# Moving the first addition of each tile's squares from GpSimd to VectorE, in a Mamba-2 block with routed experts

## What is computed

```
xn = layernorm(x)
z, xBC, dt = split(xn @ in_proj_w.T)             # 1024, 1280, 16 columns
xBC = silu(conv_b + 4-tap causal convolution of xBC)
x_, B, C = split(xBC);  dt = softplus(dt + dt_bias)
y = scan over chunks (decays from dt and A_log)  + x_ * D_skip
y = y * silu(z)
y = y * rsqrt(mean(y*y over its 1024 columns) + 1e-5) * norm_w
out = x + y @ out_proj_w.T + top-2-of-8 experts of xn
```

## Time and profile before

| | |
|---|---|
| median of three runs | 690.48 us |
| the profiled execution | 691.86 us, its span 689.9 us, granted TensorE clock 0.981 of full |
| PE busy | 641.2 us, 93% |
| PEld busy | 527.4 us, 76% |
| DVE busy | 504.3 us, 73% |
| ACT busy | 374.7 us, 54% |
| POOL busy | 295.8 us, 43% |
| chain that ended last | PE 60%, DVE 16%, issue 8%, DMA 7%, ACT 4%, POOL 3% |

### The profile page before, as it was taken

The page is one execution under the profiler, slowest core; times in us unless marked ns, Lnnn a source line. Parts: engine busy times, 40 slices in busy tenths (PEclk is TensorE's granted clock), DMA queues, the critical chain, the costliest instruction groups (busy, mean ns, idle before and its releaser), DMA issues.

```text
span 689.9 us, 12665 instructions
## 1 busy us (share of the span) xinstructions
PE 641.2 (93%) x4215; PEld 527.4 (76%) x4216; DVE 504.3 (73%) x1098; ACT 374.7 (54%) x787; POOL 295.8 (43%) x210
## 2 busy tenths in 40 slices
PE   4898799999999999999999989999798999999991
PEld 3897677878779777787877967677477888899981
DVE  6898677877977887787797788899976644444430
ACT  4778855563763755557376373638246444444441
POOL 2002235525354444553535425331327566656641
PEclk9999999999999999999999999999999999999997
DMA  8682014304222330420422203083866676667763
GB/s 263 218 311 96 1 32 153 103 22 153 72 83 81 104 124 31 153 102 23 153 69 86 97 29 130 1 281 108 271 210 98 119 123 122 122 119 124 127 98 46
DMA packets 31826, 80.38 MB, mean 117 GB/s; under 512 B 4768, under 2 KB 10016, under 8 KB 29600
## 3 DMA queue, kind: packets, MB, share of 16 engines
q1 hardware_dynamic: 22640, 57.97, 25.4%
q0 software_dynamic: 9136, 21.76, 17.3%
HBM read 59.93 MB, written 19.79 MB: 116 GB/s over the span
## 4 chain that ended last, share of the span: by engine, by line
PE 60%; DVE 16%; issue 8%; DMA 7%; ACT 4%; POOL 3%; SPq 1%; DVEq 0%; POOLq 0%; ACTq 0%
PE pi L1484 17%; PE po L1523 10%; PE pg L1705 10%; PE pd L1718 7%; DVE xs L972 5%; PE py L1586 3%; PE py L1579 3%; DMA m<-cs_d 2%; PE px L1688 2%; PE pxb L1570 2%; DVE y L1255 2%; PE pxb L1601 1%; DMA out<-yo,idx 1%; DVE xs L987 1%; PE phs L1728 1%
## 5 line engine op out<-in xcount | busy, mean ns | idle before, releaser
L1484 PE MATMUL pi<-xh,whl 128*128 128x256 f32 x1152 | 166.3, 287 | 1.8 <-DVE zs L978 1.3
L1484 PEld LDWEIGHTS pi<-xh,whl 128*128 128x128 f32 x1152 | 147.5, 190 | 4.6 <-issue 2.4
L972 DVE SCALAR_TENSOR_TENSOR xs<-raw,conv_w,xs 128x256 f32<-128x256 f32 x240 | 111.0, 527 | 12.1 <-ACT xs L664 12.0
L1523 PE MATMUL po<-wo,y 128*128 128x512 f32 x256 | 114.6, 601 | 0.4 <-DVE y L1267 0.4
L1484 PE MATMUL pi<-xl,whl 128*128 128x256 f32 x576 | 92.1, 282 | 0.0
L1523 PEld LDWEIGHTS po<-wo,y 128*128 128x128 f32 x256 | 48.0, 192 | 55.3 <-issue 55.1
L562 POOL DMA_INDIRECT out<-yo,idx x39 | 62.1, 1593 | 60.4 <-ACT yo L830 29.8
L689 ACT ACTIVATE m<-m,cs_tok 128x128 f32<-128x128 f32 x256 | 79.8, 390 | 0.5
L1484 PEld LDWEIGHTS pi<-xl,whl 128*128 128x128 f32 x576 | 78.9, 189 | 0.0
L1705 PE MATMUL pg<-ew,xgh 128*128 x312 | 65.1, 351 | 0.0
L528 POOL TENSOR_TENSOR carry<-carry,cd 128x1024 f32<-128x1024 f32 x14 | 27.5, 1967 | 81.9 <-PE py L1579 81.9
(11 more groups left out here) (221 smaller groups left out, 1167.8 us busy)
## 6 DMA issues: line engine op xcount, KB each, us to landing
m<-cs_d SPq DMA_DIRECT2D x16, 1024.0 KB, 5.8
e<-cs_d SPq DMA_DIRECT2D x30, 256.0 KB, 4.4
ew<-in_w_gu SPq DMA_DIRECT2D x8, 768.0 KB, 7.9
w_as_read<-in_w_in SPq DMA_DIRECT2D x9, 512.0 KB, 8.9
res<-in_x SPq DMA_DIRECT2D x16, 256.0 KB, 3.8
out<-o SPq DMA_DIRECT2D x15, 256.0 KB
xin<-in_x SPq DMA_DIRECT2D x6, 512.0 KB, 3.9
xn_d<-xin SPq DMA_DIRECT2D x6, 512.0 KB, 2.8
```

The costliest lines, as they stand in the source:

```text
L972: dve.scalar_tensor_tensor(out=xs[par][:, b, :], in0=raw[:, b, k:k + GT], scalar=conv_w[:, b, k:k + 1], in1=xs[par][:, b, :], op0=ALU.mult ...
L1484: mm = pe.matmul(bank[:, hf, :], whl[:, weight(g, n), lo, k, hf * P:(hf + 1) * P], xx[:, k, :], start=k3 == 0, stop=k3 == 11)
L1523: mm = pe.matmul(po[:, :], y[:, b, :], wo[:, b, :], start=b == 0, stop=b == XB - 1)
```

## The change

GpSimd's list loses the wait for `ysqd` and the first of the three additions (L499); `sums` begins with the wait for `tree` at 3t + 1. VectorE's list gets both right behind `decayed(0)` of tile t, for t from 1 to 13, for the squares of tile t - 1. Operands, semaphore and count are the same.

```diff
@@ gpsimd
             def sums(t):
-                pool.wait_ge(ysqd, t + 1)
-                pool.tensor_tensor(ysq[:, 0:4, :], ysq[:, 0:4, :], ysq[:, 4:8, :], ALU.add).then_inc(tree, 1)
                 pool.wait_ge(tree, t * 3 + 1)
                 pool.tensor_tensor(ysq[:, 0:2, :], ysq[:, 0:2, :], ysq[:, 2:4, :], ALU.add).then_inc(tree, 1)
                 pool.wait_ge(tree, t * 3 + 2)
@@ vector
                 if 0 < t < T - 2:
                     decayed(0)
+                    dve.wait_ge(ysqd, t)
+                    dve.tensor_tensor(ysq[:, 0:4, :], ysq[:, 0:4, :], ysq[:, 4:8, :], ALU.add).then_inc(tree, 1)
                 if c == 1 and prepares:
                     time_steps(g + 2, 0, 10)
```

## The result

The changed kernel takes 694.66 us (median of five runs, 691.67 to 697.20) against 690.48 us before. The ratio is 1.0072 with an interval of 1.0037 to 1.0107: slower by 0.7%, some 5 us. I had forecast no difference, 690.4 us, and the measured median lies above the range.

A forecast was written before the change was run, and what follows sets the result against it. TensorE was taken as the bound, except in tiles 12 and 13, where VectorE makes it wait. Terms +0.3 (even) +0.3 (odd) -0.7 (tiles 12 and 13) = -0.1 us gave 690.4 us, range 687.4 to 694.2.

The forecast's parts named there:

- The even tiles: Even tiles to 10: later sum and earlier S cancel; waits 0 to 0.2 us or none, +0.3 us in all.
- S + 2.77: S is the start of decayed(0); in even tiles GpSimd's third addition completes tree 2.77 us after it.
- a relief of 1.1 to 1.7 us: VectorE's taps in even tiles get back 1.13 us (2, 6, 8) or 1.7 us (4, 10) without GpSimd's additions.
- The odd tiles: Odd tiles to 11: late sum hidden by 0.7 us, shifted steps cost TensorE about 0.05 us each, +0.3 us in all.
- 0.85 us of idle time: Odd tiles, VectorE: idle 0.45 us before decayed(1) and 0.40 us before own(0), taken to cover the 0.60 us shift.
- second rival: Odd tiles: GpSimd's two additions and VectorE's small steps delay each other more, 0.45 us a tile; 693.5 us, chance 0.18.
- Tiles 12 and 13: VectorE makes TensorE wait there; the squares come 0.27 and 0.47 us earlier, together -0.7 us.
- third rival: Tiles 12 and 13 come clean: clock stays up, xdt wait may go; 2.5 us gained, 688 us, chance 0.13.
- first rival: No relief of the taps: TensorE waits 1.13 us for tree in seven tiles, 7.9 us; 698.3 us, chance 0.07.
- the fourth: Even tiles: VectorE work slips behind GpSimd's gate, xdt 1.05 us late in five tiles; 695.7 us, chance 0.04.

The follow-up runs named there:

- kernel with the odd tiles alone: Against the kernel before, the addition of the squares is VectorE's only in odd tiles 1 to 11, GpSimd's elsewhere; ratio 1.0124.
- the one with only the steps split: The kernel before with only three of the ten small steps (L938) moved to the later group behind finish, GpSimd keeping all additions; ratio 1.0010.
- kernel with 128 columns: The kernel before, nothing moved, plus a useless VectorE reduction of 128 columns behind decayed(0) in odd tiles 1 to 11; ratio 1.0010.
- kernel with the reduction of 1024 columns: The kernel before, nothing moved, plus a useless VectorE reduction of 1024 columns behind decayed(0) in odd tiles 1 to 11; ratio 1.0099.

## Why the prediction was wrong

**The even tiles: right.** I had the addition at 0.69 us, the sum at S + 2.77, a relief of 1.1 to 1.7 us and a wait of 0 to 0.2 us. Measured are 0.67 us, S + 2.62 and waits of that size; tiles 2 to 10 are 0.1 us longer in all, where my term was +0.3 us.

**The odd tiles: the step that failed.** I had written that the steps move by 0.60 us, at the most by 1.4 us, and set this against 0.85 us of idle time before `decayed(1)` and `own(0)`. The shift was inside that bound, 1.13 us. The error is the step "that is 1.4 us against the 0.85 us of cover", from which I had `own(0)` over 0.6 us later and `diag(1)` about 0.05 us: it treats what stands behind the shift as idle time only. I had asked what the steps suffer beside GpSimd's two additions and not what they are pushed into. GpSimd's next instruction is the 1.9 us decay of the carry, tied to TensorE and so not moved; the last step had ended 0.5 us ahead of it. The rows needed for this were at hand: the multiplication's line is the one GpSimd waits longest for the earlier trace rows, and I had used the same exclusion in the taps. The price of one step held is 1.81 against 0.19 us, 1.6 us on VectorE, of which 1.03 us reaches TensorE in tile 7. The six odd tiles together make 6.6 us in place of my 0.3: `own(0)` was 1.7 us later in tile 7, not 0.6.

That exclusion is what the Trainium skill ("SBUF — State Buffer", section "Who interferes with whom") describes, and the trace agrees: the later instruction waits out the whole of the earlier one, whatever its own size. I had applied it to the partners that the change names and not to the one next to them. My second rival had the right place and the right victim, `diag(1)` in the odd tiles, but another cause, GpSimd's two additions, and so too small a price: 0.45 us a tile. These additions have their share all the same: the held L924 is 0.54 us of the 1.13. By estimate from the rows of before, a shift of 0.60 us alone would have had the last step start at 267.91 in tile 7, 0.08 us ahead of the decay at 267.99. That was not run.

**Tiles 12 and 13: right in kind, too small.** I had -0.7 us; the trace has -3.3 us. It is two things. In tile 12 the wait of 1.83 us for `decayed(0)` became two, as forecast:

```profile
415.16 1.16 PE L1579 MATMUL py<-xs,carry 128*128 128x128 f32 x8 [0.22 <-DVE e L1243]
417.19 0.35 PE L1529 MATMUL pk<-ones,ysq 128*128 128x1 f32 x2 [0.87 <-POOL ysq L501]
```

but they add to 1.1 us, not to 1.6. The first six taps take 2.45 us instead of 3.94, `decayed(0)` starts 17.4 us into the tile instead of 19.0, which is 1.6 us earlier where I had 1.4, and the sum is there 2.61 us behind it instead of 2.85. So the squares start 0.6 us earlier, where I had 0.27. In tile 13 the wait of 0.67 us is gone and the squares wait for nothing. The rest is what the third rival had: the window from 403 to 434 us now has its clock at 1.00, and `diag(0)` takes 1.09 us instead of 1.83:

```profile
403.00:434.00 31.00, 29.57 (x210) 22.72 (x209) 27.22 (x65) 17.90 (x40) 10.62 (x7) 1.00 0.23 75
```

and with it went the 1.05 us wait for `xdt`. But this part does not belong to the change for certain. The kernel with the odd tiles alone and the one with only the steps split have nothing moved in tiles 12 and 13; there too the clock stayed up, and the two tiles took 58.8 and 59.1 us together, against 60.8 before and 57.5 after. By these two the moved addition is worth 1.3 to 1.6 us, and 1.8 to 2.1 us are the difference between an execution with the lower clock in tile 12 and one without. Whether the move makes the lower clock rarer is open: the profiled executions of all five kernels with the addition moved in these tiles kept the clock up, of the five without it only two did, and each kernel has one profile.

**The sum.** -0.1 us was forecast; with the measured terms it is +6.6 (odd) + 0.1 (even) - 1.5 (tiles 12 and 13, without the clock's part) = +5.2 us or +0.75%, and with all of the 3.3 us it is +3.4 us or +0.5%. The runs say +0.72%, and their interval holds both. The first rival, the relief that isn't there, did not occur; nor did the fourth.

**What the profiled executions hid.** The sum is far from the -0.2 us between the two profiled times. One of them drew 2.5 us less before tile 1 and the other the lower clock in tile 12. The first lies ahead of the changed code; the second was also seen in two other kernels with nothing moved in tile 12, those with the reductions.

## What to carry to other kernels

Where VectorE and GpSimd both read SBUF, a step's cushion is not the idle time behind it but the distance to GpSimd's next long instruction: past that point a 0.2 us step cost here nearly that instruction's whole duration (1.81 of 1.98 us), and a cushion of 0.3 to 0.5 us decided 6.6 us. Before moving or adding work on either engine, list for each instruction behind it which one of the other engine it will now meet, also those that the change doesn't touch. And a change spread over alternate tiles is two changes: the same two lines gave 0.9973 in the even tiles with tile 13 (nothing of it from tiles 2 to 10) and 1.0124 in the odd ones.

## What the runs showed of the hardware that I had not expected

- Smallness is no protection, nor is having one input. In tile 1 of the changed kernel the held step is one of 128 by 32 with a single input, and it is held as long as the one in tile 7 (VectorE, then GpSimd):

```profile
92.90 1.82 DVE L936 TENSOR_SCALAR step_acc<-step_s 128x32 f32<-128x32 f32 x1
...
92.75 1.93 POOL L526 TENSOR_TENSOR carry<-carry,cd 128x1024 f32<-128x1024 f32 x1 [1.15 <-PE py L1579]
```

- It is the order of starting that counts: in tile 7 the first of the three L938 began at 268.97, 0.01 us ahead of the multiplication, and took its 0.19 us; the one behind it took 1.81 us. In tile 1 of the kernel with 128 columns the last of the three starts at 96.73, 0.10 us ahead of the multiplication, and takes its 0.19 us too.
- A wait of about 2 us doesn't by itself tell what the clock does. Before, the granted clock fell to its lower level in tile 12 from 414.0 us on, behind the wait of 1.83 us; in the kernel with the odd tiles alone TensorE waited 1.99 us at the same place, and the sixteen matmuls behind it took 1.09 us. In the kernel with the reduction of 1024 columns it waited the same 1.99 us there, and they took 1.77 us, at a granted clock of 0.55 (417.9 to 420.9 us). Odd tiles alone, then 1024 columns:

```profile
418.48 1.16 PE L1587 MATMUL py<-xs,carry 128*128 128x128 f32 x8 [1.99 <-DVE e L1250]
...
419.69 1.09 PE L1594 MATMUL py<-m,xdt 128*64 128x128 f32 x16
```

```profile
416.71 1.16 PE L1583 MATMUL py<-xs,carry 128*128 128x128 f32 x8 [1.99 <-DVE e L1246]
...
417.92 1.77 PE L1590 MATMUL py<-m,xdt 128*64 128x128 f32 x16
```

What decides between the two levels was not tried and stays open.
